# A degree-8 node recursion evaluated in baby and giant steps, with the cube of the node operator built on the chip

## The reference, cut to what matters

```python
h = jnp.einsum('bnd,ed->bne', x, fc_in_w) + fc_in_b
alph = jax.nn.sigmoid(alpha_train)[:, None]
w_eff = w * jnp.clip(d, 0.0, 1.0) @ w.T
dt = 1 / 8
def euler_step(h, _):
    ax = jnp.einsum('nm,bmd->bnd', adj, h)
    f = alph * 0.5 * (ax - h) + h @ w_eff - h + x0
    return (h + dt * f, None)
h, _ = jax.lax.scan(euler_step, h, None, length=8)
x = _layernorm(x + h)
```

## Time and profile before

| | us |
|---|---|
| median of 3 runs | 826.01 (824.46 to 826.44) |
| span of the profiled execution, first to last instruction | 830.8 |
| TensorE busy | 697.2 (84%) |
| VectorE busy | 606.6 (73%) |
| ScalarE busy | 391.9 (47%) |
| GpSimd busy | 334.2 (40%) |
| chain that ended last, TensorE's share | 59% |

### The profile page before, as it was taken

One profiled execution on the slowest core, in us unless ns is written; L12 is line 12 of the kernel. 1 busy time (PEld: TensorE's weight loads), 2 busy tenths in 40 slices (PEclk: granted clock), 3 DMA queues, 4 the chain that ended last, 5 costly groups with the idle time before them and its releaser, 6 DMA issues.

```text
span 830.8 us, 10324 instructions
## 1 busy us (share of the span) xinstructions
PE 697.2 (84%) x3366; PEld 578.5 (70%) x3366; DVE 606.6 (73%) x1213; ACT 391.9 (47%) x853; POOL 334.2 (40%) x264
## 2 busy tenths in 40 slices
PE   3877889998999999897599699989999999867462
PEld 2645578886887888766577478868878878656441
DVE  6658465578569788988966845886498797898454
ACT  3432237543633656524846277354626557327321
POOL 1458015643556425422252248244564246121201
PEclk9869799999999999998889889999999999989666
DMA  7000010000000000001100020000000000000101
GB/s 174 3 0 1 0 52 1 2 1 0 1 2 0 2 1 1 1 1 51 30 23 1 27 75 2 1 1 1 2 1 1 1 1 1 1 0 1 51 1 50
DMA packets 22603, 11.72 MB, mean 14 GB/s; under 512 B 2954, under 2 KB 22026, under 8 KB 22548
## 3 DMA queue, kind: packets, MB, share of 16 engines
q1 hardware_dynamic: 22548, 11.00, 5.1%
HBM read 6.80 MB, written 4.19 MB: 13 GB/s over the span
## 4 chain that ended last, share of the span: by engine, by line
PE 59%; DVE 21%; ACT 8%; POOL 7%; issue 4%; DMA 1%; DVEq 0%; ACTq 0%; POOLq 0%
PE bank L1074 28%; PE bank L1245 15%; PE bank L1244 11%; POOL ZL L465 5%; PE bank L1232 3%; DVE Y L967 3%; DVE stats L894 3%; ACT ZH L540 3%; DVE F L976 2%; POOL small L487 2%; ACT X L691 2%; PE bank L1220 1%; ACT Y L540 1%; DVE F L996 1%; DVE Y L994 1%
## 5 line engine op out<-in xcount | busy, mean ns | idle before, releaser
L465 POOL TENSOR_TENSOR ZL<-F,ZH 128x512 fp32r<-128x512 f32 x112 | 160.9, 1469 | 188.1 <-ACT ZH L540 188.1
L1245 PE MATMUL bank<-ZL,BTH 128*128 128x512 f32 x576 | 211.7, 398 | 0.0
L1244 PE MATMUL bank<-ZH,BTH 128*128 128x512 f32 x432 | 172.9, 400 | 9.9 <-POOL ZL L465 9.9
L540 ACT ACTIVATE Y<-bank 128x384 f32<-128x384 f32 (+1 forms) x352 | 146.2, 465 | 36.6 <-PE bank L1074 26.8
L967 DVE SCALAR_TENSOR_TENSOR Y<-F,cols,Y 128x512 f32<-128x512 f32 x112 | 136.1, 1267 | 16.2 <-ACT Y L540 15.7
L540 ACT ACTIVATE ZH<-F 128x512 fp32r<-128x512 f32 x112 | 64.5, 624 | 165.4 <-PE bank L1245 102.9
L1245 PEld LDWEIGHTS bank<-ZL,BTH 128*128 128x128 f32 x576 | 109.2, 190 | 26.1 <-issue 0.4
L976 DVE SCALAR_TENSOR_TENSOR F<-bank,cols,Y 128x512 f32<-128x512 f32 x128 | 91.3, 741 | 46.3 <-PE bank L1245 46.1
L487 POOL TENSOR_TENSOR small<-small,minus_half 128x16 f32<-128x16 f32 x16 | 47.4, 2962 | 185.0 <-DVE small L912 185.0
L1244 PEld LDWEIGHTS bank<-ZH,BTH 128*128 128x128 f32 x432 | 81.9, 189 | 35.0 <-issue 16.0
L1074 PE MATMUL bank<-QH,TH 128*128 128x384 f32 x192 | 67.1, 350 | 4.3 <-ACT Y L540 3.9
(11 more groups left out here) (244 smaller groups left out, 1379.4 us busy)
## 6 DMA issues: line engine op xcount, KB each, us to landing
X<-in_x SPq DMA_DIRECT2D x16, 256.0 KB, 4.1
out_x<-F SPq DMA_DIRECT2D x16, 256.0 KB, 3.0
F<-in_adj SPq DMA_DIRECT2D x1, 1024.0 KB, 5.6
Y<-in_L_gnn_W SPq DMA_DIRECT2D x1, 448.0 KB
Y<-in_L_gnn_w_neigh SPq DMA_DIRECT2D x2, 64.0 KB, 4.7
Y<-in_L_gnn_w_loop SPq DMA_DIRECT2D x2, 64.0 KB, 3.6
b_row<-in_L_gnn_b SPq DMA_DIRECT2D x2, 64.0 KB, 4.0
...
```

The costliest lines, as they stand in the source:

```text
L465: g.tensor_tensor(lo, whole, raw(hi), ALU.subtract).then_inc(pool_done[s], 1)
L540: return A.activation(out_, in_, ACT.Copy, **more)
L1244: T.matmul(bank[s][a][:, :], *operands(a, m, BTH, ZH), start=False, stop=False)
L1245: last = T.matmul(bank[s][a][:, :], *operands(a, m, BTH, ZL), start=False, stop=m == NB - 1)
```

## The change

The nine coefficients are grouped by three: the output is W0 + L^3 (W1 + L^3 W2), with W_p the sum over j = 0, 1, 2 of (L^j x) Q_{3p+j}.

- In the preparation three new stages run: `w.lmat` builds L, its parts, and its transpose in RH/RL; `w.r2` and `w.r3` multiply it by L (48 matmuls of 512 columns each), so that RH/RL holds the transposed cube. `w.powers` now waits for `w.r3`, and `w.edges` is behind `w.r2` in the order.
- Per group, `step1` and `step2` compute L x and L^2 x (32 matmuls each, with B as before); ScalarE's `scaled` copy prepares the -c term. `tz.b` transposes both for batch b (8 transposes), `lot.b` sums three products in PSUM for each node block (9 matmuls of 384 columns, 4 blocks) and gives W0 to X, W1 to F and W2 to ZH/ZL. `giant1` and `giant2` multiply by the cube (48 matmuls of 512 columns each), with an addition on VectorE after each; between them `split3` makes the parts again.
- local, lot.l.a and euler.k are gone; Y is smaller, and some scratch areas move.
- The normalized X of layer 0 now holds the 1 that t1 and the low part added as a bias: GpSimd has one more small operation (`plus_one`), and VectorE's pieces a multiply-add.
- The order of the stages is written anew.

```diff
@@ sizes and areas
-        Y = [sb(f"Y{s}", [P, LOT * NB * GB * D]) for s in range(STREAMS)]
+        Y = [sb(f"Y{s}", [P, 2 * NB * GB * D]) for s in range(STREAMS)]
+        YR = [twin(f"YR{s}", [Y[s]], F32R) for s in range(STREAMS)]
+        Z = [twin(f"Z{s}", [ZH[s], ZL[s]]) for s in range(STREAMS)]
+        RH = sb("RH", [P, NB, N], F32R)
+        RL = sb("RL", [P, NB, N], F32R)
...
@@ orders
-        prepare = """w.adj w.low w.w0 w.v 0.x0 0.t0 0.neigh1 0.conv1 w.edges w.powers w.one_hot 0.triple 0.pair2
-            w.l2_mean w.weights w.picked w.soft 0.neigh2 w.q 0.stats.0 w.end 0.norm.0 0.t1""".split()
...
+        prepare = """w.adj w.low w.w0 w.v 0.x0 0.t0 w.lmat 0.neigh1 w.r2 0.conv1 w.edges w.r3 w.powers w.one_hot 0.triple
+            0.pair2 w.l2_mean w.weights w.picked w.soft 0.neigh2 w.q 0.stats.0 w.end 0.norm.0 0.split1""".split()
+        in_turn = """1.x0 0.step1 1.t0 0.t1 1.neigh1 0.split2 0.step2 1.conv1 1.triple 0.tz.0 0.tz.1 0.lot.0 1.pair2
+            0.tz.2 0.lot.1 0.tz.3 0.lot.2 1.neigh2 0.lot.3 1.stats.0 0.giant1 0.split3 1.norm.0 1.split1 1.step1 1.t1
+            0.giant2 1.split2 1.step2 0.stats.1 0.norm.1 1.tz.0 1.tz.1 1.lot.0 0.t2 0.l2.0 0.l2.1 1.tz.2 1.lot.1
+            0.l2.2 0.l2.3 0.stats.2 1.tz.3 1.lot.2 0.norm.2 0.x3 1.lot.3 0.gather 1.giant1 1.split3 0.qv 0.score
+            1.giant2 0.spread 0.wout 1.stats.1 0.scatter 1.norm.1 1.t2 0.stats.3 1.l2.0 1.l2.1 0.norm.3 +0.x0 +0.t0
+            1.l2.2 1.l2.3 1.stats.2 +0.neigh1 1.norm.2 1.x3 1.gather 1.qv 1.score +0.conv1 1.spread +0.triple +0.pair2
+            1.wout +0.neigh2 +0.stats.0 1.scatter 1.stats.3 +0.norm.0 +0.split1 1.norm.3""".split()
@@ GpSimd
+                if i == 0:
+                    gp.wait_ge(pool_done[s], after(pool_steps, turn, "shift0"))
+                    g.tensor_scalar(sm[:, 0, :], sm[:, 0, :], 1.0, None, ALU.add).then_inc(pool_done[s], 1)
+            def split3(turn, s):
+                for a in range(NB):
+                    gp.wait_ge(act_done[s], after(act_steps, turn, "giant1_hi", a))
+                    low_part(s, z2(ZL[s], a), F[s][:, a, :, :], z2(ZH[s], a))
...
@@ ScalarE
+            def w_r(stage):
+                ac.wait_ge(w_pe_done, after(w_pe_steps, 0, stage, NB - 1))
+                for a in range(NB):
+                    copy(RH[:, a, :], w_bank[a][:, :]).then_inc(w_act_done, 1)
...
+            def scaled(s, out_, in_, a):
+                A.activation(out_, in_, ACT.Copy, scale=c_neg[:, a:a + 1]).then_inc(act_done[s], 1)
+            def split1(turn, s):
+                ac.wait_ge(dve_done[s], after(dve_steps, turn, "x0", NB * GB // 2 - 1))
+                ac.wait_ge(act_done[s], after(act_steps, turn, "x0", NB * GB // 2 - 1))
+                for a in range(NB):
+                    copy(z2(ZH[s], a), X[s][:, a, :, :]).then_inc(act_done[s], 1)
+                    scaled(s, F[s][:, a, :, :], X[s][:, a, :, :], a)
+            def lot(turn, s, b):
+                for a in range(NB):
+                    from_psum(turn, s, f"lot{b}", a, ZH[s][:, a, b, :], bank[s][a][:, 2 * D:3 * D])
+                    copy(w_parts(s, a, b), bank[s][a][:, 0:2 * D].rearrange("p (k d) -> p k d", d=D)).then_inc(
+                        act_done[s], 1)
+            def split3(turn, s):
+                ac.wait_ge(pe_done[s], after(pe_steps, turn, "giant1", NB - 1))
+                for a in range(NB):
+                    ac.wait_ge(dve_done[s], after(dve_steps, turn, "giant1", a))
+                    copy(z2(ZH[s], a), F[s][:, a, :, :]).then_inc(act_done[s], 1)
...
@@ VectorE
+            def step(turn, s, stage, scaled, state):
+                for a in range(NB):
+                    dv.wait_ge(act_done[s], after(act_steps, turn, scaled, a))
+                    dv.wait_ge(pe_done[s], after(pe_steps, turn, stage, a))
+                    v.scalar_tensor_tensor(state[:, a, :, :], wide(s, a), c_r[:, a:a + 1], state[:, a, :, :],
+                                           ALU.mult, ALU.add).then_inc(dve_done[s], 1)
+            def giant2(turn, s):
+                for a in range(NB):
+                    dv.wait_ge(pe_done[s], after(pe_steps, turn, "giant2", a))
+                    v.tensor_tensor(F[s][:, a, :, :], wide(s, a), X[s][:, a, :, :], ALU.add).then_inc(dve_done[s], 1)
+                    block_stats(turn, s, 1, a, "giant2")
...
@@ TensorE
+            def by_l():
+                for a in range(NB):
+                    terms = []
+                    for q in range(NB):
+                        terms += three(l_hi[:, q, block_of(a)], l_lo[:, q, block_of(a)], RH[:, q, :], RL[:, q, :])
+                    products(w_bank[a][:, :], terms).then_inc(w_pe_done, 1)
+            def w_r2():
+                pt.wait_ge(w_dve_done, after(w_dve_steps, 0, "r_lo", NB - 1))
+                by_l()
+            def w_r3():
+                pt.wait_ge(w_dve_done, after(w_dve_steps, 0, "src_col"))
+                by_l()
             def w_powers():
+                pt.wait_ge(w_dve_done, after(w_dve_steps, 0, "r3_lo", NB - 1))
...
+            def step1(turn, s):
+                by_b(turn, s, "step1", "x1_hi", (pool_done, pool_steps, "x1_lo"), NB, left(s))
+            def tz(turn, s, b):
+                for j, (state, what) in enumerate(((F, "step1"), (X, "step2"))):
+                    begin(turn, s, f"tz{b}", j, (dve_done, dve_steps, what, NB - 1))
+                    for a in range(NB):
+                        last = T.transpose(bank[s][bank_of(f"tz{b}", j)][:, block_of(a)], state[s][:, a, b, :],
+                                           ident[:, :])
+                    last.then_inc(pe_done[s], 1)
+            def lot(turn, s, b):
+                for a in range(NB):
+                    terms = []
+                    for j in range(LOT):
+                        hi, lo = (TH[s][:, b, :], TL[s][:, b, :]) if j == 0 else (zt(s, b, j - 1, 0), zt(s, b, j - 1, 1))
+                        part = slice(j * LOT, (j + 1) * LOT)
+                        terms += three(hi[:, block_of(a)], lo[:, block_of(a)], QH[:, part, :], QL[:, part, :])
...
+            def giant(turn, s, stage, hi_step, lo_step):
+                for m in range(NB):
+                    for a in range(NB):
...
+                        for i, (lhs_t, rhs) in enumerate(three(RH[:, m, block_of(a)], RL[:, m, block_of(a)],
+                                                               z2(ZH[s], m), z2(ZL[s], m))):
+                            last = T.matmul(bank[s][a][:, :], lhs_t, rhs, start=m == 0 and i == 0,
+                                            stop=m == NB - 1 and i == 2)
+                        if m == NB - 1:
+                            last.then_inc(pe_done[s], 1)
```

More of the change, by code:

```diff
@@ L257, in build_program, with bank_of @@
             ("conv1", "h1_hi"), ("l2", "l2"), ("qv", "v"))})
-        for l, ks in lots:
-            last_reader[f"lot{l}"] = (act_done, act_steps, f"lot{l}")
-            for k in ks:
-                last_reader[f"euler{k}"] = (dve_done, dve_steps, f"euler{k}")
+        last_reader.update({what: (dve_done, dve_steps, f"{what}_lo") for what, _ in lots})
+        last_reader.update({what: (dve_done, dve_steps, what) for what in ("step1", "step2", "giant1", "giant2")})
+        first_bank = {"tz1": 2, "tz3": 2}
+        def bank_of(stage, i):
+            return (first_bank.get(stage, 0) + i) % 4
         bank_user = {}
@@ L525, in w_end @@
                 gp.wait_ge(w_act_done, after(w_act_steps, 0, "q_t", LOTS - 1))
-            stages = {"x0": x0, "neigh1": neigh1, "conv1": conv1, "stats": stats_of, "split": split_state,
-                      "euler": euler,
+            stages = {"x0": x0, "neigh1": neigh1, "conv1": conv1, "stats": stats_of, "split1": split1,
+                      "split2": split2, "split3": split3,
                       "x3": x3, "one_hot": w_one_hot, "q": w_q, "end": w_end}
@@ new lines, in step2, with tz @@
+            def step2(turn, s):
+                step(turn, s, "step2", "scaled2", X[s])
+            def tz(turn, s, b):
+                for j in range(2):
+                    low(turn, s, f"tz{b}", f"tz{b}_hi", j, zt(s, b, j, 1), zt(s, b, j, 0),
+                        bank[s][bank_of(f"tz{b}", j)][:, :])
+            def lot(turn, s, b):
+                for a in range(NB):
+                    low(turn, s, f"lot{b}", f"lot{b}", a, ZL[s][:, a, b, :], ZH[s][:, a, b, :],
+                        bank[s][a][:, 2 * D:3 * D])
@@ L1310, in t2, with giant1, giant2 @@
+            def giant1(turn, s):
+                giant(turn, s, "giant1", "lot3_hi", (dve_done, dve_steps, "lot3_lo"))
+            def giant2(turn, s):
+                giant(turn, s, "giant2", "giant1_hi", (pool_done, pool_steps, "giant1_lo"))
             def t2(turn, s):
```

260 lines of the change are left out of this document (147 added, 113 removed).

## The result

The changed kernel takes 887.7 us (median of 4 runs, 886.8 to 888.6) where the kernel before takes 826.1 beside it: a ratio of 1.071, interval 1.067 to 1.075. It is 7.1% slower. The prediction said 2% slower (844, range 800 to 863): the sign was right, the time lies 25 above the range. The profiled execution has a span of 885.0, 54.2 more than before.

The account below looks back on a forecast made before the run. TensorE was taken to bound the dense parts, chains over other engines the tails, one chain the preparation. 830.8 + 36.3 - 2x11.6 + 5.8 - 1.3 = 848.4 span, less 4.8: 844 us, 2% slower, range 800 to 863.

Parts of the forecast that it names:

- Preparation, +36.3: One-time preparation: the new products join its chain, so X0 is ready at 157.0 and not 120.7, 36.3 us later.
- The waits of the dense part: Dense part: TensorE's waits from walking the engines' queues, stage by stage, the longest 7.5 and 7.3 us.
- Losses 49: Each dense part: 49 us of waits, pacing and low clock, the clock falling only after waits of 7 us or more.
- the 199: Each dense part: TensorE's work after the change, 237 less 38 us.
- the 4.8: Whole kernel: the median taken 4.8 us below the profiled span, as for the kernel before.
- Rival 3: Dense parts: the clock falls after waits of 3 to 5 us too, 9 a part, 862 us; with above 858, chance 0.14.
- The price of a cold stage: 32 matmuls following a wait of 8.73 us take 10.25 for 7.5, read as the low clock's cost, 2.75.
- where nothing runs beside them: Preparation's four GpSimd splits, 1.24 us each, taken as running alone; 1.25 used for the pacing splits.
- Tail, +5.8: Between turns: 3.4 us won after the scatter, gather 5.1 later at its end; next X0 103.9 after the scatter, +5.8.
- Last tail, -1.3: Last turn's tail: 3.4 us won and only norm.3, 2.1, added, so 1.3 shorter.
- Rival 1: Dense parts: TensorE's work stays the bound, each falls by 38, median 787 us; with results up to 822, chance 0.25.
- Rival 2: Preparation: better hidden, only its matmuls count, +24, 831 us; at the forecast's lower end, no chance of its own.

Follow-up runs that it names:

- e3: The changed kernel without w.r2 and w.r3, the giant steps multiplying by L and not its cube: 858.4 us, ratio 1.033 to the kernel before.
- e1: The changed kernel with 1.norm.0 and 1.split1 moved ahead of 0.giant1 and 0.split3: 867.8 us, ratio 1.043 to the kernel before.
- e9: The changed kernel with 0.norm.1 moved from ahead of 1.tz.0 to behind 1.lot.0: 867.8 us, ratio 1.050 to the kernel before.
- e2: The changed kernel with unused matmuls put into nine of TensorE's waits a turn, waits kept: 856.1 us, ratio 1.031 to the kernel before.
- e12: e7 with longer fill-ins, plus 34 before the tail's neigh1 in a bank free in time: 768.2 us, ratio 0.927 to the kernel before.
- e5: The changed kernel with only the tail's stage order put back as in the kernel before: 874.2 us, ratio 1.052 to the kernel before.
- e4: The changed kernel with the same stages in a new order, the tail as in the kernel before: 785.0 us, ratio 0.946 to that kernel.
- e7: e4 with w.r3 ahead of the edge matmuls and unused fill-in matmuls in some TensorE waits: 772.7 us, ratio 0.931 to the kernel before.

## Why the prediction was right or wrong

- *Preparation, +36.3: measured +28.9.* The chain was right, link by link (e3: the cube's products are on it). Two links were priced at the low clock and ran at full: neigh1 7.55 for 10.2 of the earlier trace rows, w.r3 11.3 for 13.5. The edges stage was about 1.5 shorter, and the remaining 1.0 is spread over small links.
- *The waits of the dense part: 41.4 forecast, 45.7 measured.* The walk through the queues held: 7.5 and 7.3 forecast for the two longest, 8.96 and 7.85 measured; step2 4.1 and 4.10; lot0 of stream 0 3.6 and 3.65; lot1 of stream 1 4.4 and 4.29; gather 1.9 and 2.01. The largest misses are score, 2.1 against 4.12, and the 1.5 at step1 of stream 1. e1 and e9 removed the two longest by the order of the stages.
- **The step that failed is the term "Losses 49" of the dense part, in its share for the low clock.** I had let TensorE fall to 1.2 GHz "after waits of 7 us and more only"; the losses beyond the waits came to 7.7, mostly pacing. Measured are 16.5 for the clock (e2, row by row) and 5.1 for the pacing of three stages (3 times 9.2 less 7.5), together 21.6, where the term had 7.7: 13.9 too little. The part came out at 269.6 and not at 248; the difference is these 13.9, 4.3 more of waits, and some 3.4 of work above the 199 (202.3 is what is left of 269.6). Of the sum: 848.4 + 21.6 + 20.3 - 7.4 (preparation) - 0.1 + 2.2 (tails) = 885.0, the span. The last 7.5 of the distance to 887.7 come from the step after the sum: I took 4.8 off the span for the median, and the median lies 2.7 above it. In each run on record an execution's time lies 1.8 to 2.0 above its own span, and the kernel before took 824.5 to 836.1 in its single executions; so the 4.8 said only that its profiled execution was a longer one.
- *Rival 3* was this mechanism, but took 9 a part and a clock of "about 0.9": the clock came out at 0.89, the price was higher, because waits of 2 us (gather, lot2, wout) and the stage behind score paid as well. Its chance of 0.14 was too low: the dense part before has hardly any wait of 2 us and more, so its clock of 0.98 said nothing against it. The Trainium skill (TensorE: Matmul & The Clock Gate, Part 4: PE-mode transpose) says that transposes do not count as activity for the clock. The runs don't bear this out: in the preparation the clock was 0.50 during 16 transposes, with no other matmul among them, and full for neigh1 right behind them, and fill-in matmuls in the waits, with the transposes as they were, gave the clock back (e2).
- *The price of a cold stage* was read from the earlier trace rows, 10.25 for 7.5. e12 shows that this stage takes 9.3 at full clock: about 1 of the 2.75 was the clock and 1.8 the splits. For a lot, which nothing paces, the price is 2.4 to 2.5. The number I used was about right, its reading was wrong. So was the reading of the earlier trace rows, "where nothing runs beside them": VectorE was busy for 68% to all of the time of those four splits. The 1.25 taken from it was right all the same (see the last section).
- *Tail, +5.8: measured +5.7.* The first cause is right: gather begins 48.3 after the scatter (forecast 47.1). That the sum is right to 0.1 is luck: by e5 the new order costs 7.7 and the rest is 2.0 less than before; I had 9.2 and 3.4, and the two errors cancel. *Last tail, -1.3: measured +0.9*: the order costs 6.2 there, with a slow scatter, where I had 2.1.
- *Rival 1* (TensorE's work stays the bound, 787) failed for this kernel, and its arithmetic for the dense parts was nearly right: in e4, the same instructions in another order, they took 224.5 and 223.4 where 221.8 was forecast. That e4's 785.0 lies so near to 787 is partly luck: its preparation grew by 30.5 and not 36.3, and its tails shrank by 3 each. *Rival 2*: its +24 is nearer to the measured 28.9 than my 36.3, because no link ran at the low clock as priced; its reason is not borne out, since e3 puts 25.8 on the two products, whose bare matmuls take 22.4, and nothing of them is hidden.
- Open: how the clock falls after a given wait is not fixed. giant2 of stream 0, behind the same wait of 2.80, took 11.3 in e4 and 12.7 in e12, and neigh1 of stream 1, behind the same 0.86, took 8.6 in e4 and 10.2 in e12, which is more than the 1.0 that the fill-ins before step1 had won just ahead of it. What decides there was not found; the price of a single stage is good to some 1.5 us.

## What to carry to other kernels

A saving on the busiest engine counts only if the order of the stages keeps it fed. In the first dense part 35 us less of TensorE work came with 31 more of waiting (45.7 for 14.4) and 13 more of slow or paced matmuls (21.6 for 8.2), until the order was written anew for the new stages (0.946 instead of 1.071). Price every wait of TensorE twice, once for its length and once for the stages behind it, also where it is only 2 to 4 us long and others follow; unused matmuls in the wait buy the second part back, if they begin at once and reach to near the end of the wait (with up to 1.8 us left behind them in e2 they did, with 3.75 left in e7 the gather behind them still took 9.2 for 7.5), and if the stage behind is not paced by its operands anyway. A one-time product of matrices is not free because the engine is partly idle there: ask which chain it joins.
